# Between a graph layer and an attention layer: when weights are loaded, who fills a row of ones, and which product comes first

## The chip, the core and the metric

One NeuronCore of a Trainium2 chip. The metric is the device time of one execution in microseconds (us). Engines: PE (TensorE), DVE (VectorE), ACT (ScalarE), POOL (GpSimd) and SP (SyncE, which here only issues DMAs).

## The reference

A network of two graph blocks on 6250 nodes with 128 features and 206,250 edges sorted by target. The first block makes a message per edge, reduces the messages of each target (sum, squares, maximum, minimum), and applies two dense layers. The second is what matters here:

```python
h = x @ gcn_w                                   # graph layer (GCN)
out = zeros.at[dst].add(h[src] * norm[:, None])
h = silu(layernorm(out + gcn_b) )               # with gamma, beta
hh = (h @ gat_w).reshape(N, 2, 128)             # attention layer (GAT), 2 heads
a_src = sum(hh * att_src, -1);  a_dst = sum(hh * att_dst, -1)
e = leaky_relu(a_src[src] + a_dst[dst])
alpha = exp(e - m[dst]) / den[dst]              # m, den: maximum and sum over the edges of a target
out = mean over heads of sum(hh[src] * alpha);  x = layernorm(x + silu(layernorm(out + gat_b)))
```

## The kernel before

Nodes lie on the free axis, padded to 6400, in the large tile `acc` of 128 features x 5 planes x 6400. The program is a row of phases, each a block of five instruction streams; between two blocks all engines meet at a barrier, and after some phases POOL clears semaphores in a small block of its own (`recycle`).

- `phase_sum` is the graph layer: it adds scaled feature rows over the edges into plane 1 of `acc`. SP loads the row starts of the edge list (`rr`, L1217) and waits for DVE, which computes from them where the irregular windows begin (`s_jt`); then SP loads the edge indices (`meta`, L1228) by which POOL gathers rows (L1256).
- `phase_gcn` is the stage changed here. It turns plane 1 into the tables of the attention layer, in 13 groups of 512 nodes (the last has 256), 4 blocks of 128 each. SP loads seven small tiles (L1521 to L1526): `gw` (the graph layer's weight), `gwT` (the attention weight, transposed), `at` (two score weights) and `gb` (bias, gamma, beta on all partitions), all on one semaphore. PE first makes the score vectors (L1533, into `PV`, a corner of the PSUM tile `AB`), that is weight times score weight, and then per group: `q` the product with `gw` (L1541), `t` a transpose, `a` the scores (L1561, L1564). DVE first fills a row of ones on partition 32 of planes 3 and 4 (L1573; the attention layer keeps its running sum there), then copies the score vectors to SBUF and adds them (L1575, L1577), and then per group: `f1` scales and adds the bias (L1586), makes the statistics (L1590, L1593) and adds epsilon to the variance (L1595); `f2` normalises (L1602 to L1611) after ACT's square root; `gg` copies scores and takes the leaky maximum (L1627). ACT makes the square root, the SiLU, copies and stores. POOL has no instruction in it.
- `phase_gat` is the attention layer itself, 2100 us of gathers and products; it starts after a barrier.

The order within a stream is written out by hand: `steps(NG, [(lag, f), ...])` calls in step i every f for group i - lag. `Chain` counts DVE's instructions on a semaphore; `ch.sync()` waits for all of them, and `ch.raises(s)` signals s by a no-op behind them (L97).

Of the kernel before, what the change touches and what calls it, by code (L numbers as in the profile page):

```python
# [9 lines left out]
ALU = mybir.AluOpType  # L10
# [32 lines left out]
class Entry:  # L43
# [15 lines left out]
    def first(self, m):  # L59

        return isinstance(self.i, int) and self.i + self.o < m
# [38 lines left out]
def build(nc, d, out, upto=99):  # L100
    with ExitStack() as top:
        def sem(name):
            return top.enter_context(nc.semaphore(name))
# [39 lines left out]
        s_pool = sem("s_pool")  # L143
        s_sync = sem("s_sync")
        s_pad = sem("s_pad")


        with ExitStack() as ph:
# [251 lines left out]
        phase_n1(nc, d, locals())  # L400
        if upto < 3:
            return
        phase_sum(nc, d, locals())
        phase_gcn(nc, d, locals())
        if upto < 5:
            return
        phase_gat(nc, d, locals())
# [369 lines left out]
def steps(n, stages, before=None):  # L777

    for i in range(n + max(lag for lag, _ in stages)):
        if before is not None and i < n:  # L780
            before(i)
        for lag, f in stages:
            if 0 <= i - lag < n:
                f(i - lag)
# [343 lines left out]
def phase_sum(nc, d, v):  # L1128
# [12 lines left out]
    with ExitStack() as ph:  # L1141
# [73 lines left out]
        @blk.sync  # L1215
        def _(e):
            e.dma_start(rr[:, :], RPD[0:(NW + 1) * WD].rearrange("(a w k) -> a w k", a=1, k=WD)[:, :, 0],  # L1217
                        allow_slow_non_contiguous=True).then_inc(l_rr, 16)
            e.wait_ge(s_jt, 1)
            j0 = entry0(e)  # L1220

            def load(x):
                k = x.slot(4)
                c = e.value_load(tb[0:1, ds(nth(e, j0, x), 1)], min_val=0, max_val=NCH - 1)
                if not x.first(4):
                    wait_sync(e, l_g[k], 64 * x.uses(4, -1), s_sync)
                    wait_sync(e, s_oh, x.at(-3), s_sync)
                e.dma_start(meta[:, k, :], d["meta"][ds(c, 1), :, :].rearrange("a p s -> (a p) s")).then_inc(l_mt[k], 16)  # L1228

            for o in range(4):  # L1230
                load(Entry(0, o))
            e.wait_ge(s_lim, 1)
            e.dma_start(WTD.rearrange("(a k) n -> a k n", a=1), wt[:, :, :]).then_inc(l_wt, 16)
            e.wait_ge(l_wt, 16)
            e.dma_start(wc[:, :, :], WTD.rearrange("k (g p) -> p k g", p=128), allow_slow_non_contiguous=True).then_inc(l_wt, 16)
            with e.bass.Fori(4, entries(e), 4, engines=bass.OrderedEngineSet([e.engine])) as i:
                for o in range(4):
                    load(Entry(i, o))
# [232 lines left out]
def phase_gcn(nc, d, v):  # L1471
# [5 lines left out]
    TAB, ADT = v["TAB"], v["ADT"]  # L1477
    NG = len(GROUPS)
    with ExitStack() as ph:
        gw = sbt(ph, "gw", [128, 128])  # L1480
        gwT = sbt(ph, "gwT", [128, 2, 128])
        at = sbt(ph, "at", [128, 2, 2])
        gb = sbt(ph, "gb", [128, 3, 128])
        vv = sbt(ph, "vv", [128, 3, 2])
        tt = sbt(ph, "tt", [128, 2, 4, 128])
        zz = sbt(ph, "zz", [128, 2, 4, 128])
# [8 lines left out]
        AB = pst(ph, "AB", [128, 512])  # L1495
        LR = [pst(ph, f"LR{k}", [128, 512]) for k in range(2)]
        PV = AB[:, 500:504]
        w = sem("m_w")
        s_o = [sem(f"m_o{k}") for k in range(4)]
        s_pv = sem("m_pv")  # L1500
        s_vv = sem("m_vv")
# [14 lines left out]
            o, n = GROUPS[g]  # L1516
            return slice(o, o + n), n, n // 128

        @blk.sync
        def _(e):  # L1520
            e.dma_start(gw[:, :], d["gcnw"]).then_inc(w, 16)  # L1521
            e.dma_start(gwT[:, :, :], d["gatwT"].rearrange("(h c) f -> c h f", h=2)).then_inc(w, 16)
            e.dma_start(at[:, 0, :], d["atts"]).then_inc(w, 16)
            e.dma_start(at[:, 1, :], d["attd"]).then_inc(w, 16)
            for k, t in enumerate(("gcnb", "gamma", "beta")):
                e.dma_start(gb[:, k, :], d[t].partition_broadcast(128)).then_inc(w, 16)  # L1526

        @blk.tensor
        def _(e):
            e.wait_ge(w, 112)  # L1530
            for h in range(2):
                for k in range(2):
                    mm = e.matmul(PV[:, 2 * k + h:2 * k + h + 1], gwT[:, h, :], at[:, k, h:h + 1], start=True, stop=True)  # L1533
            mm.then_inc(s_pv, 1)

            def q(g):
                c, n, nb = cols(g)
                if g >= 2:
                    e.wait_ge(s_f1, g - 1)
                for b in range(nb):  # L1540
                    mm = e.matmul(Q[g % 2][:, b * 128:(b + 1) * 128], acc[:, 1, c.start + b * 128:c.start + (b + 1) * 128],  # L1541
                                  gw[:, :], start=True, stop=True)
                mm.then_inc(s_q, 1)

            def t(g):
                c, n, nb = cols(g)
                e.wait_ge(s_h, g + 1)
                if g >= 1:
                    e.wait_ge(s_c1, g)
                for b in range(nb):  # L1550
                    mm = e.transpose(HT[:, b * 128:(b + 1) * 128], ts[:, g % 4, b, 0:128], ident[:, :])
                mm.then_inc(s_t, 1)

            def a(g):
                c, n, nb = cols(g)
                e.wait_ge(s_c1, g + 1)
                e.wait_ge(s_vv, 1)
                if g >= 1:
                    e.wait_ge(s_g, g)
                for b in range(nb):  # L1560
                    e.matmul(AB[:, b * 4:b * 4 + 4], acc[:, 1, c.start + b * 128:c.start + (b + 1) * 128],  # L1561
                             vv[:, 0:2, :].rearrange("p k h -> p (k h)"), start=True, stop=True)
                for h in range(2):
                    mm = e.matmul(LR[h][0:1, 0:n], vv[:, 2, h:h + 1], acc[:, 1, c], start=True, stop=True)  # L1564
                mm.then_inc(s_ab, 1)

            steps(NG, [(0, q), (2, t), (3, a)])

        @blk.vector
        def _(e):  # L1570
            ch = Chain(e, s_v)
            e.wait_ge(w, 112)
            ch(e.memset(acc[32:33, 3:5, :], 1.0))  # L1573
            e.wait_ge(s_pv, 1)
            ch(e.tensor_copy(vv[:, 0:2, :].rearrange("p k h -> p (k h)"), PV[:, :]))  # L1575
            ch.sync()
            ch(e.tensor_tensor(vv[:, 2, :], vv[:, 0, :], vv[:, 1, :], ALU.add))  # L1577
            ch.raises(s_vv)

            def f1(g):  # L1580
                c, n, nb = cols(g)
                q = g % 2
                e.wait_ge(s_q, g + 1)
                for b in range(nb):
                    o = c.start // 128 + b
                    ch(e.scalar_tensor_tensor(tt[:, q, b, :], Q[q][:, b * 128:(b + 1) * 128], dinv[:, o:o + 1],  # L1586
                                              gb[:, 0, :], ALU.mult, ALU.add))
                ch.sync()
                for b in range(nb):
                    ch(e.bn_stats(bn[:, b, :], tt[:, q, b, :]))  # L1590
                ch.sync()
                for b in range(nb):
                    ch(e.bn_aggr(mv[:, q, b, :], bn[:, b, :]))  # L1593
                ch.sync()
                ch(e.tensor_scalar(rs[:, q, 0:nb], mv[:, q, 0:nb, 1], EPS, None, ALU.add))  # L1595
                ch.raises(s_f1)

            def f2(g):
                c, n, nb = cols(g)
                q = g % 2  # L1600
                e.wait_ge(s_rs, g + 1)
                ch(e.reciprocal(rs[:, q, 0:nb], rs[:, q, 0:nb]))  # L1602
                ch.sync()
                for b in range(nb):
                    ch(e.scalar_tensor_tensor(tt[:, q, b, :], tt[:, q, b, :], mv[:, q, b, 0:1], gb[:, 1, :],
                                              ALU.subtract, ALU.mult))
                ch.sync()
                if g >= 2:
                    e.wait_ge(s_h, g - 1)
                for b in range(nb):  # L1610
                    ch(e.scalar_tensor_tensor(zz[:, q, b, :], tt[:, q, b, :], rs[:, q, b:b + 1], gb[:, 2, :],  # L1611
                                              ALU.mult, ALU.add))
                ch.raises(s_f2)

            def gg(g):
                c, n, nb = cols(g)
                q = g % 2
                e.wait_ge(s_ab, g + 1)
                AV = AB[:, 0:4 * nb].rearrange("p (b k) -> p b k", k=4)
                q = g % 4  # L1620
                if g >= 4:
                    e.wait_ge(s_o[q], 32 * (g // 4))
                ch(e.tensor_copy(ts[:, q, 0:nb, 128:130], AV[:, :, 0:2]))
                ch(e.tensor_copy(adt[:, q, 0:nb, :], AV[:, :, 2:4]))
                e.wait_ge(s_lr, g + 1)
                for h in range(2):
                    ch(e.tensor_tensor(acc[0:1, 3 + h, c], lr[0:1, h, 0:n], LR[h][0:1, 0:n], ALU.max))  # L1627
                ch.raises(s_g)

            steps(NG, [(1, f2), (0, f1), (3, gg)])  # L1630

        @blk.scalar
        def _(e):
# [619 lines left out]
```

## Time and profile before

| | |
|---|---|
| median of 3 runs | 5772.62 us (5770.69 to 5776.23) |
| the profiled execution | 5773.65 us |
| its span, first to last instruction | 5771.7 us |
| mean granted clock of TensorE | 0.947 |
| PE, DVE, ACT, POOL busy | 88%, 83%, 50%, 67% |
| graph layer (`phase_sum`) | 2485 to 3385 us |
| stage changed (`phase_gcn`) | 3387 to 3520 us |
| attention layer | 3524 us to about 5625 us |

A row of the timeline gives the start and the length of an instruction (or of several alike, xN, merged), engine and line, the tiles written and read, and in brackets how long the engine stood idle before and what released it. SPq is SP's DMA issue. PE records: an fp32 product of one 128x128 block appears as two or more records. The granted clock is 1.0 at 2.4 GHz and 0.5 at 1.2 GHz.

### The profile page before, as it was taken

To read this page: it belongs to the slowest core of one execution; us is meant where nothing else is said; L and a number is where in the kernel's file an instruction comes from. 1 tells how busy PE (TensorE), PEld (TensorE's weight loads), DVE (VectorE), ACT (ScalarE), POOL (GpSimd) and SP (SyncE) were. 2 spreads that over 40 slices of the span, in tenths; PEclk is the share of its full clock that TensorE was granted. 3 is DMA by queue.
4 is the path that set the end of the run, shared out by engine and by line. 5 is a ranking of instruction groups with operands and counts; after the bars stand their busy time and mean duration, and the time that the engine had idled before them with its cause. 6 is when DMAs were issued, how large, how long until landed. Compare 5 with 4: busy or idle time off the path is not lost. (4 is left out here: it accounts for less than half of the span.)

```text
span 5771.7 us, 176467 instructions
## 1 busy us (share of the span) xinstructions
PE 5106.0 (88%) x41872; PEld 4051.2 (70%) x42482; DVE 4775.1 (83%) x12693; ACT 2880.1 (50%) x6715; POOL 3884.4 (67%) x3976
## 2 busy tenths in 40 slices
PE   3999999999999997968888866999999999999993
PEld 3888888888888886447777754666666666666663
DVE  4999999999999997767777756888888888888887
ACT  1565666656665654123333334555555555555556
POOL 2777777777777774047777724777777777777772
PEclk7999999999999998969888877999999999999996
DMA  6666666666666664322222212222222222222221
GB/s 156 160 159 159 157 158 156 159 156 158 157 157 157 158 157 119 99 53 54 54 54 53 54 33 43 54 53 53 54 53 53 53 53 53 53 53 53 53 53 48
DMA packets 667245, 544.72 MB, mean 94 GB/s; under 512 B 365794, under 2 KB 544171, under 8 KB 666853
## 3 DMA queue, kind: packets, MB, share of 16 engines
q0 software_dynamic: 126336, 262.13, 19.1%
q1 hardware_dynamic: 415050, 163.69, 12.4%
q10 hardware_dynamic: 125724, 117.57, 7.8%
q14 instruction: 108, 0.88, 0.1%
q8 instruction: 27, 0.44, 0.0%
HBM read 517.22 MB, written 25.61 MB: 94 GB/s over the span
## 5 line engine op out<-in xcount | busy, mean ns | idle before, releaser
L1766 POOL DMA_INDIRECT Gt<-TAB,metat x1632 | 1597.2, 979 | 646.9 <-issue 496.4
L559 POOL DMA_INDIRECT G<-Atab,ms x1616 | 1575.6, 975 | 576.9 <-issue 460.3
L1256 POOL DMA_INDIRECT Gc<-XS,metac x672 | 645.3, 960 | 241.8 <-issue 189.0
L1806 DVE SCALAR_TENSOR_TENSOR M<-neqt,Gt 128x256 f32<-128x256 f32 x816 | 311.0, 422 | 309.0 <-DMA Gt<-TAB,metat 308.8
L663 ACT COPY BS<-BK 128x512 f32<-128x512 f32 x808 | 465.6, 576 | 198.9 <-PE BK L752 191.1
L1401 ACT COPY acc<-CP 128x300 f32<-128x300 f32 x630 | 269.5, 428 | 555.1 <-PE CP L1439 552.4
L606 DVE TENSOR_TENSOR_SCAN ST<-mm,ST,ET 128x512 f32<-128x512 bf16 x404 | 516.7, 1279 | 0.1
L608 DVE TENSOR_TENSOR_SCAN ST<-mm,ST,ET 128x512 f32<-128x512 bf16 x404 | 506.9, 1255 | 0.0
L702 PE MATMUL Z<-WB,ZR 128*128 128x128 f32 x3232 | 429.3, 276 | 66.8 <-DVE ZR L577 66.6
L752 PE MATMUL BK<-ident,ST 128*128 128x128 f32 x3232 | 485.1, 273 | 2.4 <-ACT BS L663 1.8
L1970 PE MATMUL SR<-P,Gt 128*128 128x128 f32 x3264 | 473.7, 288 | 0.0
L1970 PEld LDWEIGHTS SR<-P,Gt 128*128 128x128 f32 x3264 | 395.8, 191 | 70.2 <-issue 70.2
L720 PE MATMUL S<-EE,oh 128*64 128x128 f32 x6464 | 442.5, 279 | 0.0
L702 PEld LDWEIGHTS Z<-WB,ZR 128*128 128x128 f32 x3232 | 428.5, 193 | 12.0
L1414 PE MATMUL OT<-acc 128*128 128x180 f32 x2100 | 431.7, 332 | 0.5 <-ACT acc L1401 0.5
L1904 ACT ACTIVATE EX<-TE,nl 128x512 f32<-128x512 f32 x408 | 294.7, 722 | 270.9 <-ACT nl L1897 140.2
L639 ACT ACTIVATE EE<-EE 128x512 f32<-128x512 f32 x404 | 255.1, 631 | 346.3 <-issue 273.1
L769 PE MATMUL S<-BS,oh 128*64 128x128 f32 x6464 | 422.5, 273 | 1.4 <-issue 1.4
L752 PEld LDWEIGHTS BK<-ident,ST 128*128 128x128 f32 x3232 | 392.6, 141 | 32.7 <-issue 2.5
L1327 DVE TENSOR_SCALAR O<-iotaD,VA 128x300 bf16<-128x300 f16 x1260 | 400.3, 322 | 1.0
L720 PEld LDWEIGHTS S<-EE,oh 128*64 128x64 f32 x6464 | 345.0, 137 | 67.7 <-issue 67.7
L1439 PE MATMUL CP<-O 128*128 128x300 bf16 x1260 | 301.2, 326 | 78.3 <-DVE O L1327 74.8
(291 smaller groups left out, 11448.5 us busy)
## 6 DMA issues: line engine op xcount, KB each, us to landing
mm<-MM ACTq DMA_DIRECT2D x404, 256.0 KB
ZR<-in_eft SPq DMA_DIRECT2D x404, 128.0 KB
dstb<-DF SPq DMA_DIRECT2D x404, 128.0 KB
Gt<-TAB,metat POOLq DMA_INDIRECT x1632
G<-Atab,ms POOLq DMA_INDIRECT x1616
ad<-ADT SPq DMA_DIRECT2D x816, 0.2 KB
WB<-Btab SPq DMA_DIRECT2D x404, 32.0 KB
Gc<-XS,metac POOLq DMA_INDIRECT x672
```

The source lines that it names most:

```text
L559: e.indirect_dma_start(G[:, k, s, :], None, Atab, bass.IndirectOffsetOnAxis(ap=ms[:, k, s:s + 1], axis=0)).then_inc(l_g[k], 16)
L606: e.tensor_tensor_scan(ST[:, q, 0, :], mm2[:, k, 0, :], ET[q][:, :], ST[:, 1 - q, 0, CH - 1:CH], ALU.mult, ALU.max)
L608: e.tensor_tensor_scan(ST[:, q, 1, :], mm2[:, k, 1, :], ET[q][:, :], ST[:, 1 - q, 1, CH - 1:CH], ALU.max, ALU.min).then_inc(s_d3, 1)
L663: e.copy(BS[:, q, a, :], BK[:, :]).then_inc(s_a2[a], 1)
L702: mm = e.matmul(Z[q][:, s * 128:(s + 1) * 128], ZR[:, k, s * 128:(s + 1) * 128], WB[:, k, :], start=True, stop=True)
L720: mm = e.matmul(S1[a * 64:(a + 1) * 64, 0:128], oh[:, k, s, :], EE[:, q, a, s * 128:(s + 1) * 128], start=(s == 0), stop=(s == 3))
L752: mm = e.transpose(BK[:, s * 128:(s + 1) * 128], ST[:, q, a, s * 128:(s + 1) * 128], ident[:, :])
L769: mm = e.matmul(S2[a * 64:(a + 1) * 64, 0:128], oh[:, k, 4 + s, :], BS[:, q, a, s * 128:(s + 1) * 128], start=(s == 0), stop=(s == 3))
L1256: e.indirect_dma_start(G[:, k, s, :], None, XS, bass.IndirectOffsetOnAxis(ap=meta[:, k, s:s + 1], axis=0)).then_inc(l_g[k], 16)
L1414: mm = e.matmul(OT[k][:, 0:DB], acc[:, 0, h * 128:(h + 1) * 128], C[k][:, h, :], start=(h == 0), stop=(h == NB - 1))
L1766: e.indirect_dma_start(G[:, k, s, :], None, TAB, bass.IndirectOffsetOnAxis(ap=meta[:, k, s:s + 1], axis=0)).then_inc(l_g[k], 16)
L1970: m = e.matmul(SR[q][:, 0:2 * W], G[:, k, s, 0:128], P[:, q, s * 128:(s + 1) * 128], start=(s == 0), stop=(s == 3))
```

## The change

The four weight tiles are allocated around both phases and loaded by SP in `phase_sum`, behind the load of the row starts. In `phase_gcn` the row of ones is filled by POOL, PE makes the first group's product before the score vectors, and DVE copies and adds these behind its first group.

```diff
@@ build
+        l_gw = sem("l_gw")
...
-        phase_sum(nc, d, locals())
-        phase_gcn(nc, d, locals())
+        with ExitStack() as mid:
+            gw = sbt(mid, "gw", [128, 128])
+            gwT = sbt(mid, "gwT", [128, 2, 128])
+            at = sbt(mid, "at", [128, 2, 2])
+            gb = sbt(mid, "gb", [128, 3, 128])
+            phase_sum(nc, d, locals())
+            phase_gcn(nc, d, locals())
@@ phase_sum, sync
             e.dma_start(rr[:, :], RPD[0:(NW + 1) * WD]...).then_inc(l_rr, 16)
+            e.dma_start(v["gw"][:, :], d["gcnw"]).then_inc(v["l_gw"], 16)
+            e.dma_start(v["gwT"][:, :, :], d["gatwT"].rearrange("(h c) f -> c h f", h=2)).then_inc(v["l_gw"], 16)
+            e.dma_start(v["at"][:, 0, :], d["atts"]).then_inc(v["l_gw"], 16)
+            e.dma_start(v["at"][:, 1, :], d["attd"]).then_inc(v["l_gw"], 16)
+            for k, t in enumerate(("gcnb", "gamma", "beta")):
+                e.dma_start(v["gb"][:, k, :], d[t].partition_broadcast(128)).then_inc(v["l_gw"], 16)
             e.wait_ge(s_jt, 1)
@@ phase_gcn
-        w = sem("m_w")
+        gw, gwT, at, gb, w = v["gw"], v["gwT"], v["at"], v["gb"], v["l_gw"]
+        s_one = sem("m_one")
...
-        @blk.sync
-        (the same seven loads)
+        @blk.gpsimd
+        def _(e):
+            e.memset(acc[32:33, 3:5, :], 1.0).then_inc(s_one, 1)
+            e.wait_ge(s_one, 1)
@@ tensor
             e.wait_ge(w, 112)
-            (the score vectors)
+            def score_vectors(): (the same)
...
-            steps(NG, [(0, q), (2, t), (3, a)])
+            def product(g):
+                q(g)
+                if g == 0:
+                    score_vectors()
+
+            steps(NG, [(0, product), (2, t), (3, a)])
@@ vector
             e.wait_ge(w, 112)
-            ch(e.memset(acc[32:33, 3:5, :], 1.0))
-            e.wait_ge(s_pv, 1)
-            ch(e.tensor_copy(vv[:, 0:2, :].rearrange("p k h -> p (k h)"), PV[:, :]))
-            ch.sync()
-            ch(e.tensor_tensor(vv[:, 2, :], vv[:, 0, :], vv[:, 1, :], ALU.add))
-            ch.raises(s_vv)
...
-            steps(NG, [(1, f2), (0, f1), (3, gg)])
+            def first(g):
+                f1(g)
+                if g == 0:
+                    (wait for s_pv, copy, add and signal as above)
+
+            steps(NG, [(1, f2), (0, first), (3, gg)])
```

DVE at the start of the stage, before:

```order
L1569 UNCONDITIONAL_BRANCH [waits barrier_Pool_Activation_PE_DVE_SP_release]
L1573 MEMSET acc 1x12800 [waits m_w]
L1575 COPY vv<-AB 128x4 [waits m_pv]
L1577 TENSOR_TENSOR vv<-vv 128x2 [waits m_v]
L97 ISA [waits m_v]
L1586 SCALAR_TENSOR_TENSOR tt<-Q,dinv,gb 128x128 [waits m_q]
```

The memset stands between the barrier and all that DVE does on a group. Now:

```order
L1591 SCALAR_TENSOR_TENSOR tt<-Q,dinv,gb 128x128 [waits m_q,l_gw]
L1591 SCALAR_TENSOR_TENSOR tt<-Q,dinv,gb 128x128 x3
L1595 BN_STATS bn<-tt 128x6 [waits m_v]
L1595 BN_STATS bn<-tt 128x6 x3
L1598 BN_AGGR mv<-bn 128x2 [waits m_v]
L1598 BN_AGGR mv<-bn 128x2 x3
L1600 TENSOR_SCALAR rs<-mv 128x4 [waits m_v]
L97 ISA [waits m_v]
L1639 COPY vv<-AB 128x4 [waits m_pv]
L1641 TENSOR_TENSOR vv<-vv 128x2 [waits m_v]
L97 ISA [waits m_v]
L1607 RECIPROCAL rs<-rs 128x4 [waits m_rs]
```

The memset is gone from DVE, and the copy and the addition stand between the first group's statistics and its reciprocal. (What is L1595 before the change is L1600 after it.) SP in the graph layer, now:

```order
L1223 DMA rrs<-RPD 1x631x1
L1225 DMA gw<-in_gcnw 128x128
L1226 DMA gwT<-in_gatwT 128x2x128
L1227 DMA at<-in_atts 128x2
L1228 DMA at<-in_attd 128x2
L1230 DMA gb<-in_gcnb 128x128
L1230 DMA gb<-in_gamma 128x128
L1230 DMA gb<-in_beta 128x128
L1198 TENSOR_LOAD jt [waits c_jt]
```

Seven issues stand between the load of the row starts and SP's wait for the table. POOL has the memset as its one instruction between two barriers.

## Rows read from the trace of the kernel before

**Rows 1.** The page: the span, and each engine's busy time

```profile
span 5771.7 us, 176467 instructions
...
PE 5106.0 (88%) x41872; PEld 4051.2 (70%) x42482; DVE 4775.1 (83%) x12693; ACT 2880.1 (50%) x6715; POOL 3884.4 (67%) x3976
```

**Rows 2.** Busy time by stretch: start:end length, PE, PEld, DVE, ACT, POOL, PEclk, DMA, GB/s

```profile
3387.00:3393.60 6.60, 0.00 (x0) 0.00 (x0) 0.00 (x0) 0.00 (x0) 0.00 (x0) 0.50 0.26 60
3393.60:3407.00 13.40, 5.49 (x24) 5.19 (x24) 10.71 (x1) 0.00 (x0) 0.00 (x0) 0.63 0.00 0
3407.00:3519.00 112.00, 77.11 (x286) 40.54 (x286) 82.14 (x331) 68.52 (x103) 0.00 (x0) 0.73 0.13 30
```

**Rows 3.** Timeline, start of attention tables: start, us, engine, line, tiles, [idle before]

```profile
3387.08 0.34 SPq L1521 DMA_DIRECT2D gw<-in_gcnw  x1
...
3389.87 0.43 SPq L1526 DMA_DIRECT2D gb<-in_beta  x1
...
3393.63 1.86 PE L1533 MATMUL AB<-at,gwT 128*128 128x1 f32 x8 [9.30 <-DMA gb<-in_beta]
...
3396.30 10.72 DVE L1573 MEMSET acc<- 1x12800 f32 x1 [11.15 <-issue]
3407.05 0.16 DVE L1575 COPY vv<-AB 128x4 f32<-128x4 f32 x1
...
3407.45 1.12 DVE L1586 SCALAR_TENSOR_TENSOR tt<-Q,dinv,gb 128x128 f32<-128x128 f32 x4
...
3409.93 0.17 DVE L1595 TENSOR_SCALAR rs<-mv 128x4 f32<-128x4 f32 x1
3410.18 0.21 ACT L1637 ACTIVATE rs<-rs 128x4 f32<-128x4 f32 x1 [58.94 <-DVEq L97]
...
3410.21 2.08 PE L1541 MATMUL Q<-gw,acc 128*128 128x128 f32 x8 [11.09 <-DVEq L97]
...
3410.42 0.18 DVE L1602 RECIPROCAL rs<-rs 128x4 f32<-128x4 f32 x1 [0.33 <-ACT rs L1637]
```

**Rows 4.** Timeline, the program's first stage: DVE beside POOL's memset

```profile
2.66 21.42 POOL L230 MEMSET acc<- 128x25600 f32 x1
14.27 10.03 DVE L304 CAST rows<-rowi 1x403 f32<-1x403 int32 x1 [14.15 <-DMA rowi<-in_lin]
24.23 0.34 DVE L305 CAST rows<-rowi 1x403 f32<-1x403 int32 x1
```

**Rows 5.** Timeline, the last stage: DVE beside a POOL operation

```profile
5743.08 1.26 POOL L2156 TENSOR_TENSOR yy<-zz,x 128x512 f32<-128x512 f32 x1 [2.91 <-ACT zz L2183]
...
5743.64 0.73 DVE L2095 TENSOR_SCALAR rs<-mv 128x4 f32<-128x4 f32 x1
...
5745.80 0.17 DVE L2095 TENSOR_SCALAR rs<-mv 128x4 f32<-128x4 f32 x1
```

**Rows 6.** Timeline, the start of the graph layer

```profile
2485.63 0.73 SPq L1217 DMA_DIRECT2D rrs<-RPD  x1
...
2485.96 0.38 POOL L1242 IOTA iotaD<- 128x300 f16 x1 [241.93 <-POOLq L789]
...
2491.29 0.47 DVE L1279 TENSOR_SCALAR rrs<-rrs 1x631 f32<-1x631 f32 x1 [4.21 <-DMA rrs<-RPD]
...
2499.30 3.92 SPq L1228 DMA_DIRECT2D metac<-in_meta  x4
```

**Rows 7.** DMA issues there: tile, queue, count, KB each, us to landing

```profile
gw<-in_gcnw SPq DMA_DIRECT2D x1, 64.0 KB, 1.8
...
gb<-in_beta SPq DMA_DIRECT2D x1, 64.0 KB, 3.7
```

**Rows 8.** Timeline, PE's row products near the end of the stage

```profile
3493.44 1.88 PE L1564 MATMUL LR<-acc,vv 128*1 128x512 f32 x4
...
3502.10 3.50 PE L1564 MATMUL LR<-acc,vv 128*1 128x512 f32 x4
```

More of the change, by code:

```diff
@@ L1479, in phase_gcn @@
     with ExitStack() as ph:
[L1480 to L1483, printed above, removed]
+        gw, gwT, at, gb, w = v["gw"], v["gwT"], v["at"], v["gb"], v["l_gw"]
         vv = sbt(ph, "vv", [128, 3, 2])
@@ L1517, in cols @@
             return slice(o, o + n), n, n // 128
-        @blk.sync
+        @blk.gpsimd
         def _(e):
[L1521 to L1526, printed above, removed]
+            e.memset(acc[32:33, 3:5, :], 1.0).then_inc(s_one, 1)
+            e.wait_ge(s_one, 1)
         @blk.tensor
@@ L1530, in _, with score_vectors @@
             e.wait_ge(w, 112)
[L1531 to L1534, printed above, removed]
+            def score_vectors():
+                for h in range(2):
+                    for k in range(2):
+                        mm = e.matmul(PV[:, 2 * k + h:2 * k + h + 1], gwT[:, h, :], at[:, k, h:h + 1], start=True, stop=True)
+                mm.then_inc(s_pv, 1)
             def q(g):
@@ L1628, in gg @@
                 ch.raises(s_g)
-            steps(NG, [(1, f2), (0, f1), (3, gg)])
+            def first(g):
+                f1(g)
+                if g == 0:
+                    e.wait_ge(s_pv, 1)
+                    ch(e.tensor_copy(vv[:, 0:2, :].rearrange("p k h -> p (k h)"), PV[:, :]))
+                    ch.sync()
+                    ch(e.tensor_tensor(vv[:, 2, :], vv[:, 0, :], vv[:, 1, :], ALU.add))
+                    ch.raises(s_vv)
+            steps(NG, [(1, f2), (0, first), (3, gg)])
         @blk.scalar
```

## The prediction

> **What bounds the kernel now.** I read the page first: engine shares of the whole span [rows 1]. PE and DVE are busy 88% and 83% of it, but the edit touches one short stage, so those shares say nothing of its worth. The busy time by stretch shows the stage [rows 2]: 6.6 us in which no engine does anything, 13.4 us in which DVE has one instruction, and then 112 us of real work on 13 groups. All engines pass a barrier at its start and at its end, so every microsecond saved in the first two stretches moves the end of the program, unless it comes back later. The timeline gives the chain of waits [rows 3]. SP issues its first weight load at 3387.08 and its last at 3389.87; PE starts at 3393.63, released by that last load; DVE's memset begins at 3396.30 and takes 10.72; then come the copy of the score vectors at 3407.05 and the first operation on a product at 3407.45. So DVE reaches its first useful work 20.4 us after SP's first issue: 6.55 (loads) + 2.67 (a wait that the trace gives to nobody) + 10.75 (memset) + 0.40 (copy and add).
>
> **The change part by part.** The sum is made against the profiled execution's own 5773.65 us; the median shown is 5772.62, 1.0 lower, and the predicted time starts from the median.
>
> *Weights loaded in the graph layer.* The seven issues leave this stage: -6.55 us, if nothing else takes their place. They are placed behind the row-start load on SP's queue and ahead of SP's wait for the window table. Here they took from 3387.08 to 3390.30 to issue [rows 3], 3.2 us; behind the row-start load, which ends at 2486.4, they end near 2489.6, and the first load of edge indices is only issued at 2499.30 [rows 6]. SP's queue is thus covered with 9.7 us to spare; without that cover each would cost its 0.46. Their transfers run beside the row-start load, for which DVE waits until 2491.29 [rows 6]. Bounds: nothing, as the first load of the seven landed in 1.8 us with six behind it, while the last needed 3.7 [rows 7]; or that DVE gets the row starts only after all seven have landed, 6.55 after 2486.4, thus 2492.9 in place of 2491.29, +1.7. I take 0, since the row-start load is first in its queue as the 1.8 us one was.
>
> *Product ahead of the score vectors.* PE's first four blocks take 2.08 us (eight records at the granted clock of 0.5, the 1.2 GHz level, like the row at 3410.21 [rows 3]; the stretch before has 0.50 too [rows 2]). With weights in place it starts with the stage, at about 3387.1, and DVE can start at about 3389.3. From there alone DVE would be 3407.45 - 3389.3 = 18.1 us early. The four score products (1.86 for eight records) run while DVE is on the first product, and the second group's products follow; both lie beside DVE's work.
>
> *Row of ones on POOL.* DVE loses 10.72 us of work, and the 2.67 before it. POOL does nothing in this stage [rows 2], and nobody waits for the row inside the stage, so its own time looks hidden. It is not. In the first stage a cast of 403 elements took 10.03 us beside POOL's memset, ending at 24.26, just after the memset's end at 24.08; the same form next to it took 0.34 [rows 4]. In the last stage a tensor_scalar of 4 elements took 0.73 beside a POOL operation that ended at 5744.34, and itself ended at 5744.37; alone it takes 0.17 [rows 5]. That instruction is the same as L1595, which closes the statistics of each group in the stage changed here: `rs<-mv`, 128x4. The Trainium skill (SBUF — State Buffer, Who interferes with whom) has this as a rule: a copy, cast or tensor_scalar in a two-port mode and a GpSimd instruction exclude each other for the whole instruction, and whichever is issued first wins; by it the change gains less than the trace of the stage alone suggests, and the two stretches agree.
>
> So POOL starts its memset when the stage starts, 0.33 after SP as in the graph layer [rows 6], at 3387.4. Its length: 25600 elements took 21.42 [rows 4], so 12800 take 10.7, to 3398.1. DVE does the four products' scaling and the statistics in 2.48 us (3407.45 to 3409.93 [rows 3]) and reaches the tensor_scalar at 3391.8. There it waits 6.3 us and ends 0.03 to 0.2 after the memset, at 3398.2. Before, it ended at 3410.10. **Gain so far: 11.9 us**, in place of 18.1. Queued behind it on DVE are the score-vector copy and all later groups; ACT's square root and PE's third product wait for it too.
>
> *Score-vector copy and add moved behind the first group.* They take 0.40 (3407.05 to 3407.45). Before, DVE waited 0.32 there for ACT's square root (3410.10 to 3410.42), which now covers most of it; with the signal to ACT ahead of them and one behind them, about 0.12 is left over: +0.1. PE needs the vectors only three steps later.
>
> *The rest.* The 112 us of 13 groups keep their order, and the end barrier finds POOL long done. Near the end of the stage PE's four row-product records took 3.50 us at the low clock, and 1.88 earlier at the high one [rows 8]; how the clock falls there once the start is different can't be read. The last two full groups and the half one wait for PE in part, which bounds a gain by 1.6 + 1.6 + 0.8 = 4 us; a loss is bounded near 0, as they already run mostly at the low clock. I take 0. Sum: -11.9 + 0.1 + 0 = **-11.8 us**: 5761.9 for a profiled execution, 5760.8 for the median.
>
> **The rivals.**
> - *Full gain.* The memset does not hold DVE up (one partition only, where rows 4 has 128; or the tensor_scalar of 4 elements is not of the kind that is held). Then DVE ends L1595 at 3389.3 + 2.65 = 3391.95: -18.0 us, 5754.6. Against it speak both stretches [rows 4, 5], of which the second is the very form. If the unexplained 2.67 us belongs to DVE's start and not to the memset, this case gives -15.4, 5757.2. Chance 0.12.
> - *The memset is longer than its row says.* On DVE the stretch from PE's start at 3393.63, on the same semaphore, to the next instruction at 3407.05 is 13.4 us, with a row of 10.72 in it [rows 3]; the row's 0.84 ns per element is also POOL's in rows 4. If POOL's real pace were 13.4 for 12800, it would end at 3400.8 and the gain be 9.2: 5763.4. Against it: POOL's row of 21.42 starts at 2.66 and the cast that it held was free at 24.26, and 26.8 us do not fit into that. The Trainium skill (VectorE: DVE Perf Modes, Zero memsets can be issued as uint32) says that a memset takes one cycle per element, and gives 0.96 GHz for VectorE: an estimate of 13.3 us, which would explain the 2.67 on DVE and says nothing of POOL's clock. Chance 0.08.
> - *A late start.* Row starts delayed by the added transfers (+1.7), or POOL or PE entering the stage 1 to 2 us later than assumed, of which only POOL's costs anything: about -10, 5762.6. Chance 0.08.
> - *Slower than before.* POOL fills one partition at the pace at which it adds two tensors, 1.26 us for 512 [rows 5], 2.5 ns per element: 31.5 us, to 3418.9. DVE would be held at L1595 until 3419, 9 us later than now: 5781.6. It decides from 22.7 us on, 1.77 ns per element. Against it: rows 4, 0.84. Chance 0.02.
> - *The change doesn't do what it says.* Nothing in the stage waits for a load any more except the weights, and they have 890 us to land; I see no way, and give it no chance of its own.
>
> **How the numbers follow.** My forecast has 0.70. Inside it lie the clock at the stage's end and how the 2250 us of attention behind it fall out, about 2 us either way. A measurement of this kernel can tell about 0.2%, 11.5 us, from no change, and the forecast of -11.8 stands almost on that bound: 0.62 of its chance is beyond it, since the clock's unknown leans to a gain. Faster: 0.70 x 0.62 + 0.12 = 0.55. Slower: 0.01, half of the last case. Same: 0.44. The range takes the forecast from -8 to -16 and reaches down to the full gain: 5754.5 to 5764.5; the slow case is left out, and about half of the long memset.
>
> **What would show it.** Right: PE's first product at 3387.1 to 3387.5 on the old scale; a POOL memset of 10.7 us from the start of the stage; one DVE tensor_scalar `rs<-mv` of about 6.4 us that ends with it, the other twelve at 0.17; seven issues in 3.3 us between the row-start load and the index loads, and the gap before the first graph-layer DVE operation still 4.2. Wrong: that first tensor_scalar at 0.17 (full gain), a memset of another length, or a stage of 112 us that is more than 2 us longer or shorter from that instruction to its end.

## The result

| | before | changed |
|---|---|---|
| median, 14 runs each | 5772.94 us (5768.49 to 5777.25) | 5759.18 us (5757.21 to 5766.00) |
| ratio | | 0.998, 95% interval 0.9973 to 0.9987 |
| the profiled execution | 5773.65 us | 5760.19 us |
| its span | 5771.7 us | 5758.1 us |

The change makes the kernel 13.8 us faster by the medians, 0.24%, and the interval of the ratio lies wholly under 1, by more than 0.1%. The forecast was 11.8 us, 5760.8. The page of the changed kernel, for [rows 1]:

```profile
span 5758.1 us, 177079 instructions
...
PE 5133.3 (89%) x42482; PEld 4048.9 (70%) x42482; DVE 4769.9 (83%) x12692; ACT 2880.2 (50%) x6715; POOL 3892.4 (68%) x3977
```

The shares of the whole span don't show the change, as expected. The timeline at the stage's start, for [rows 3]. Columns as there: start, us, engine, line, tiles, in brackets the idle time before. What was L1595, L1602, L1575 and L1586 is now L1600, L1607, L1639 and L1591:

```profile
3384.02 0.34 DVE L1345 TENSOR_TENSOR acc<-acc,OT 128x180 f32<-128x180 f32 x1
3386.32 10.76 POOL L1530 MEMSET acc<- 1x12800 f32 x1 [6.98 <-SPq L1491]
...
3386.36 2.05 PE L1547 MATMUL Q<-gw,acc 128*128 128x128 f32 x8 [2.81 <-PEq L795]
...
3388.53 1.12 DVE L1591 SCALAR_TENSOR_TENSOR tt<-Q,dinv,gb 128x128 f32<-128x128 f32 x4 [4.16 <-PE Q L1547]
...
3391.01 6.10 DVE L1600 TENSOR_SCALAR rs<-mv 128x4 f32<-128x4 f32 x1
3397.15 0.16 DVE L1639 COPY vv<-AB 128x4 f32<-128x4 f32 x1
...
3397.54 0.17 DVE L1607 RECIPROCAL rs<-rs 128x4 f32<-128x4 f32 x1
...
3402.58 0.17 DVE L1600 TENSOR_SCALAR rs<-mv 128x4 f32<-128x4 f32 x1
```

POOL's memset and PE's first product start together, 1.96 us after the graph layer's last DVE operation has ended. DVE is on the first product at 3388.53 and at its tensor_scalar at 3391.01. That one instruction is held: it takes 6.10 us and ends at 3397.11, 0.03 after POOL's memset (3397.08); the next of its form takes 0.17. The whole line says the same (minimum, median and maximum in ns):

```profile
L1600 DVE TENSOR_SCALAR rs<-mv x13: 169/170/6098, 3391.0 to 3483.4; 128x4 f32<-128x4 f32 x12, 128x2 f32<-128x2 f32 x1
```

I measure the stage's start from the graph layer's last DVE instruction (start) to the first reciprocal: before 3384.80 to 3410.42, 25.62 us; now 3384.02 to 3397.54, 13.52 us. That is 12.1 of the 13.6 us by which the spans differ. The graph layer ends 0.78 earlier in this execution, and the rest falls behind the stage. Its end and the start of the attention layer, changed kernel:

```profile
3489.09 3.57 PE L1570 MATMUL LR<-acc,vv 128*1 128x512 f32 x4
...
3497.03 3.57 PE L1570 MATMUL LR<-acc,vv 128*1 128x512 f32 x4
...
3503.72 1.02 PE L1570 MATMUL LR<-acc,vv 128*1 128x256 f32 x4
...
3511.29 0.11 DVE L1787 MEMSET zw<- 128x64 uint32 x1 [5.10 <-PEq L1491]
```

and the kernel before:

```profile
3509.43 3.25 PE L1564 MATMUL LR<-acc,vv 128*1 128x512 f32 x4
...
3515.88 1.86 PE L1564 MATMUL LR<-acc,vv 128*1 128x256 f32 x4
...
3524.24 0.11 DVE L1773 MEMSET zw<- 128x64 uint32 x1 [5.05 <-PEq L1479]
```

From the first reciprocal to that memset of the attention layer it is 113.75 us now and 113.82 before, although the granted clock at the stage's end did move: the last full group's row products now took 3.57 (granted clock 0.50) and the half group's 1.02 (0.96), where they took 3.25 (0.57) and 1.86 (0.50). Counted from the first reciprocal, the last full group's end 0.80 us later than before, and the half group's, which come last, 0.12 earlier. From that memset to the end of the span it is 2246.8 against 2247.5. The start of the graph layer, for [rows 6]:

```profile
2485.68 0.73 SPq L1223 DMA_DIRECT2D rrs<-RPD  x1
...
2486.46 3.88 SPq L1225 DMA_DIRECT2D gw<-in_gcnw  x1
...
2491.31 0.48 DVE L1291 TENSOR_SCALAR rrs<-rrs 1x631 f32<-1x631 f32 x1 [4.17 <-DMA rrs<-RPD]
...
2493.03 0.43 SPq L1230 DMA_DIRECT2D gb<-in_beta  x1
...
2499.31 3.88 SPq L1240 DMA_DIRECT2D metac<-in_meta  x4
```

DVE has the row starts 5.63 us after their issue, against 5.66 before, and the index loads are issued at 2499.31 against 2499.30. So the added loads cost nothing there. But the first of them kept SP's queue for 3.88 us, and the last was issued at 2493.03, not before 2489.6.

### The profile page after: what moved, and what is told of

The parts are those of the page before. It is cut to its first block and busy times, and to the rows that moved or that the text cites. A ratio compares the mean times of both kernels' runs of the same rounds, so it can differ in the third digit from the quotient of the medians.

```text
span 5758.1 us, 177079 instructions
## 1 busy us (share of the span) xinstructions
PE 5133.3 (89%) x42482; PEld 4048.9 (70%) x42482; DVE 4769.9 (83%) x12692; ACT 2880.2 (50%) x6715; POOL 3892.4 (68%) x3977
```

## The experiments

Twelve runs, each a set of executions or a single one, on three chips. On two of these chips the whole program took about 7930 us, with the runs of one kernel spread over 1%; there only the inside of the stage can be read, and its start agrees to 0.01 us with the first comparison: the changed kernel has 13.52 us from the graph layer's end to the first reciprocal in both. The third chip was like that of the first comparison (before: 5762.75 us, 9 executions). On it ran the two-input epsilon for the third time, "order back" and the two kernels that combine the two-input epsilon with a part undone. "Distance" below is always that from the graph layer's last DVE instruction to the first reciprocal. The kernel before was profiled only in the first comparison.

| kernel | distance, us | to the attention layer, us |
|---|---|---|
| before | 25.62 | 113.82 |
| changed | 13.52 | 113.75 |
| changed, again | 13.52 | 113.09 |
| two-input epsilon (three runs) | 7.59, 7.58, 7.58 | 114.09, 114.23, 113.11 |
| memset in 13 pieces | 7.58 | 113.19 |
| loads back in the stage | 13.81 | 112.72 |
| early loads alone | 19.15 | 113.64 |
| early loads, memset halved between DVE and POOL | 12.49 | 113.77 |
| two-input epsilon, POOL copies | 13.62 | 113.24 |
| order back | 13.41 | 113.29 |
| two-input epsilon, order back | 9.10 | 112.11 |
| two-input epsilon, loads in the stage | 13.82 | 112.93 |

The second column, from the first reciprocal to the attention layer's first memset, spreads by 2 us, and by 1.1 us within one kernel (the two-input epsilon); I see no edit that it follows.

**The changed kernel again.**

> The changed kernel again, as the reference for the runs beside it. Expected 13.8 us under the kernel before (5772.94 to 5759.18 in the runs already seen), with the first tensor_scalar of the stage held for about 6.1 us until POOL's memset ends.

Measured: 7917.3 us against 7932.4, ratio 0.9983 with an interval of 0.9959 to 1.0007, which takes in both the expected gain and none; the tensor_scalar took 6.10 us again.

**Two-input epsilon.** POOL's memset stays whole; only the held instruction changes its form.

```diff
-ch(e.tensor_scalar(rs[:, q, 0:nb], mv[:, q, 0:nb, 1], EPS, None, ALU.add))
+ch(e.scalar_tensor_tensor(rs[:, q, 0:nb], ones[:, 0:nb], EPS, mv[:, q, 0:nb, 1], ALU.mult, ALU.add))
```

> Epsilon is added by an instruction with two inputs in SBUF (ones times epsilon, plus the variance) in place of the tensor_scalar, in all 13 groups. Theory A (the tensor_scalar was held because its form and POOL's memset exclude each other, while a two-input instruction is not held by a POOL instruction that only writes): the instruction takes about 0.2 us in the first group too, the memset runs on beside it, and the kernel is 6 us faster than the changed one, 20 us under before. Rival B (any DVE instruction that writes to SBUF after the statistics is held by the memset, or the first one is late for a reason that has nothing to do with POOL): it still takes about 6 us, and the time stays at 13.8 us under before.

Timeline of this kernel:

```profile
4794.44 0.34 DVE L1345 TENSOR_TENSOR acc<-acc,OT 128x180 f32<-128x180 f32 x1
4796.73 10.76 POOL L1530 MEMSET acc<- 1x12800 f32 x1 [6.96 <-SPq L1491]
...
4801.43 0.16 DVE L1600 SCALAR_TENSOR_TENSOR rs<-ones,mv 128x4 f32<-128x4 f32 x1
...
4802.03 0.17 DVE L1608 RECIPROCAL rs<-rs 128x4 f32<-128x4 f32 x1
```

The instruction that adds epsilon takes 0.16 us while the memset runs on for another 5.9. Theory A holds: what is held is the form, not whatever DVE does there. End to end 7923.6 us, ratio 0.999 (0.9967 to 1.0014): the expected 20 us (0.9975) lie inside the interval, and so does no gain.

**Memset in pieces.**

```diff
-e.memset(acc[32:33, 3:5, :], 1.0).then_inc(s_one, 1)
-e.wait_ge(s_one, 1)
+for g in range(NG):
+    e.wait_ge(s_f1, g + 1)
+    e.memset(acc[32:33, 3:5, cols(g)[0]], 1.0).then_inc(s_one, 1)
+e.wait_ge(s_one, NG)
```

> POOL's memset in 13 pieces of 2x512, each after the signal that closes a group's statistics. Theory A: each piece takes 0.9 to 1.0 us and lies beside DVE instructions with two inputs, so that no tensor_scalar is held; the first one takes 0.17 us and the kernel is 6 us faster than the changed one, 20 us under before. Rival B (late for a reason other than POOL): the first tensor_scalar still takes 6 us and the time is that of the changed kernel. In-between: if pieces hit a copy or the two-input instructions too, some of the 13 groups get up to 1 us longer each, and up to all of the 6 us is lost.

```profile
4782.43 0.34 DVE L1345 TENSOR_TENSOR acc<-acc,OT 128x180 f32<-128x180 f32 x1
...
4789.41 0.17 DVE L1602 TENSOR_SCALAR rs<-mv 128x4 f32<-128x4 f32 x1
...
4789.69 0.94 POOL L1532 MEMSET acc<- 1x1024 f32 x1 [11.93 <-DVEq L97]
...
4790.01 0.17 DVE L1609 RECIPROCAL rs<-rs 128x4 f32<-128x4 f32 x1
```

Here the held instruction is untouched, and with POOL idle when it comes it takes 0.17; the 13 of its line take 0.17 on average, so no piece holds any of them. Both ways to part the two give the same 5.93 to 5.94 us. End to end 7928.7 us, ratio 0.9994 (0.9973 to 1.0015), unclear again; the expected 20 us would be 0.9975, near the interval's lower end.

**Loads back in the stage.** The seven loads leave `phase_sum` and are issued by SP in `phase_gcn`; POOL's memset and the order stay.

```diff
@@ phase_sum, sync
-e.dma_start(v["gw"][:, :], d["gcnw"]).then_inc(v["l_gw"], 16)
...
@@ phase_gcn
+@blk.sync
+def _(e):
+    e.dma_start(gw[:, :], d["gcnw"]).then_inc(w, 16)
...
```

> Only the loads are undone: SP loads the seven tiles in the stage again, POOL's memset and the new order stay. PE then starts 6.55 us later, at 3392.9 on the changed kernel's scale, DVE reaches the tensor_scalar at about 3397.6, and POOL's memset ended at 3397.08. Theory A: the loads were hidden behind the hold but for 0.7 us, so the time is 13 us under before. Rival C (the loads carry their own 6.5 us of the gain): 7.3 us under before.

```profile
4797.36 0.34 DVE L1339 TENSOR_TENSOR acc<-acc,OT 128x180 f32<-128x180 f32 x1
...
4799.65 10.76 POOL L1533 MEMSET acc<- 1x12800 f32 x1 [6.95 <-POOLq L795]
...
4805.89 2.07 PE L1550 MATMUL Q<-gw,acc 128*128 128x128 f32 x8 [9.01 <-DMA gb<-in_beta]
...
4810.56 0.17 DVE L1603 TENSOR_SCALAR rs<-mv 128x4 f32<-128x4 f32 x1
...
4811.17 0.17 DVE L1610 RECIPROCAL rs<-rs 128x4 f32<-128x4 f32 x1
```

The weights arrive 6.2 us after the stage's start, PE and DVE are late by all of it, and it costs 0.29 us: DVE reaches the tensor_scalar 0.15 after POOL's memset has ended. Under the hold the early loads were worth 0.3 us of the stage, not 6.5. (End to end 7930.9 us, ratio 0.9997, 0.998 to 1.0015, which tells nothing.)

**Two-input epsilon, a second time.**

> The kernel with the two-input epsilon once more, because in the earlier call the whole program took 7930 us on its chip with runs spread over 1%, against 5773 us, and 6 us can't be seen there. Inside the stage the runs agreed to 0.01 us: from the graph layer's last DVE instruction to the first reciprocal 25.62 us in the kernel before, 13.52 in the changed one, 7.59 here. Theory A (what the stage gains arrives at the end of the program): 12.1 + 5.9 plus the 0.8 to 1.5 us that the changed kernel gained outside the stage, so 18 to 20 us under before, on a chip as in the first comparison. Rival (the attention layer gives some back): 14 us or less.

7912.3 us, ratio 0.9982 (0.9962 to 1.0003): the distance is 7.58 again. On these two chips the ratios of the kernels without the hold (0.999, 0.9994, 0.9982) all lie nearer to 1 than the expected 0.9975. Each interval still takes 0.9975 in, and whether the stage's gain arrives at the end there is not shown.

**Early loads alone.** DVE's memset is back, ahead of everything, and so are copy and addition; PE makes the score vectors first; POOL has nothing.

```diff
@@ vector
 e.wait_ge(w, 112)
+ch(e.memset(acc[32:33, 3:5, :], 1.0))
+e.wait_ge(s_pv, 1)
+ch(e.tensor_copy(vv[:, 0:2, :]..., PV[:, :]))
...
-steps(NG, [(1, f2), (0, first), (3, gg)])
+steps(NG, [(1, f2), (0, f1), (3, gg)])
@@ tensor
+score_vectors()
-steps(NG, [(0, product), (2, t), (3, a)])
+steps(NG, [(0, q), (2, t), (3, a)])
```

> Only the early loads of the change: DVE's memset, then the score vectors' copy, then the first group, and PE's score vectors first, as in the kernel before. Measured from the graph layer's last DVE instruction to the first reciprocal (25.62 us before). Theory D1 (the memset occupies DVE for 13.4 us although its row says 10.72): 19.1 us, so 6.5 under before. Theory D2 (the memset takes 10.72 and 2.67 is a late start that belongs to the wait for the weights): 16.4, so 9.2 under before. In either case the row reads 10.72.

```profile
4793.49 0.34 DVE L1345 TENSOR_TENSOR acc<-acc,OT 128x180 f32<-128x180 f32 x1
...
4795.82 1.84 PE L1535 MATMUL AB<-at,gwT 128*128 128x1 f32 x8 [2.81 <-PEq L795]
...
4798.51 10.72 DVE L1576 MEMSET acc<- 1x12800 f32 x1 [4.68 <-issue]
4809.27 0.16 DVE L1578 COPY vv<-AB 128x4 f32<-128x4 f32 x1
...
4812.64 0.18 DVE L1605 RECIPROCAL rs<-rs 128x4 f32<-128x4 f32 x1 [0.33 <-ACT rs L1640]
```

19.15 us, as theory D1 gives. The weights are long there, yet the memset's row still begins 2.69 us after PE's, and 13.45 us pass from PE's start to the copy. The late start does not belong to the wait for the weights. Early loads alone save 6.5 us of the stage. End to end 7918.9 us, ratio 0.9978 (0.9955 to 1.0001).

**Memset halved.** As the run above, with `acc[32:33, 3, :]` on DVE and `acc[32:33, 4, :]` on POOL.

> As the run with early loads alone, but DVE fills half of the row (6400 elements) and POOL the other half at the same time. Same distance, to the first reciprocal. Theory D1 (a memset costs DVE 1.04 us per 1000 elements): 6.7 us in place of 13.4, so 12.4 us. Theory D3 (10.72 by its row for 12800, and a fixed late start of 2.67 at the stage's beginning): 5.4 + 2.7, so 13.7 us. Both kernels' POOL part ends before DVE's tensor_scalar and holds nothing; should it hold DVE's memset, DVE ends 5.4 us later than under D1.

```profile
4823.73 0.34 DVE L1345 TENSOR_TENSOR acc<-acc,OT 128x180 f32<-128x180 f32 x1
4826.03 5.42 POOL L1530 MEMSET acc<- 1x6400 f32 x1 [7.06 <-SPq L1491]
...
4826.07 1.84 PE L1539 MATMUL AB<-at,gwT 128*128 128x1 f32 x8 [2.81 <-PEq L795]
4827.42 5.39 DVE L1580 MEMSET acc<- 1x6400 f32 x1 [3.35 <-issue]
...
4832.85 0.16 DVE L1582 COPY vv<-AB 128x4 f32<-128x4 f32 x1
...
4836.22 0.18 DVE L1609 RECIPROCAL rs<-rs 128x4 f32<-128x4 f32 x1 [0.33 <-ACT rs L1644]
```

The row is half as long (5.39), and so is the "late start", 1.35 us in place of 2.69. A fixed late start would have kept 2.7. From PE's start to the copy it is 6.78 us for 6400 elements and 13.45 for 12800: 1.04 ns for each further element, of which the row shows 0.83. The distance, 12.49, is theory D1's 12.4. The two memsets ran side by side without holding each other. (One run, 7961.5 us.)

**POOL reads.** The two-input epsilon kernel, with a POOL copy in place of the memset:

```diff
-e.memset(acc[32:33, 3:5, :], 1.0).then_inc(s_one, 1)
+e.tensor_copy(acc[32:33, 3:5, :], ones[32:33, 0:1].unsqueeze(2).to_broadcast([1, 2, NP])).then_inc(s_one, 1)
```

> The two-input epsilon kernel, with POOL filling the row by a copy that reads a tile of ones, in place of a memset that reads nothing. Its length is unknown: 10.7 us at one element per cycle, up to 31.5 at POOL's pace with two inputs. Theory A (an instruction with two SBUF inputs and a POOL instruction that reads SBUF exclude each other): the instruction that adds epsilon, 0.16 us beside the memset, is held until POOL's copy ends, and the stage gets longer than the changed kernel's. Rival B2 (two-input instructions are never held by POOL's work of this kind): 0.16 us and 7.6 us to the first reciprocal as in the kernel with the memset.

```profile
4781.79 0.34 DVE L1345 TENSOR_TENSOR acc<-acc,OT 128x180 f32<-128x180 f32 x1
...
4784.11 10.84 POOL L1530 COPY acc<-ones 1x12800 f32<-1x12800 f32 x1 [6.99 <-SPq L1491]
...
4786.29 1.13 DVE L1591 SCALAR_TENSOR_TENSOR tt<-Q,dinv,gb 128x128 f32<-128x128 f32 x4 [4.16 <-PE Q L1547]
...
4788.77 6.20 DVE L1600 SCALAR_TENSOR_TENSOR rs<-ones,mv 128x4 f32<-128x4 f32 x1
...
4795.41 0.17 DVE L1608 RECIPROCAL rs<-rs 128x4 f32<-128x4 f32 x1
```

The same instruction that took 0.16 beside a memset now takes 6.20 and ends with POOL's copy. The first operation of the group, whose large input is in PSUM, is not held (1.13 for four, as ever). So the form that escapes a POOL write does not escape a POOL read. In this run both instructions also read the tile `ones`, so that the shared tile could be the cause. The last stage of the kernel before speaks against it. There POOL reads `tt` and `tu`, DVE reads another buffer of `tt` and `gb`, and four two-input instructions take 1.83 us beside POOL and 1.14 with POOL idle:

```profile
5738.91 1.26 POOL L2148 TENSOR_TENSOR tt<-tt,tu 128x512 f32<-128x512 f32 x1 [3.09 <-ACT tu L2170]
...
5739.27 1.83 DVE L2120 SCALAR_TENSOR_TENSOR tt<-tt,mv,gb 128x128 f32<-128x128 f32 x4
...
5754.63 1.14 DVE L2120 SCALAR_TENSOR_TENSOR tt<-tt,mv,gb 128x128 f32<-128x128 f32 x4
```

I had left the length open and expected the stage to become longer than the changed kernel's; it is by 0.1 us, since the copy takes 10.84. (One run, 7922.1 us.)

**Two-input epsilon, a third time**, now on a chip like the first.

> The two-input epsilon kernel a third time, for the end-to-end time. If the chip is like the one of the first comparison: 18 to 20 us under before. If it is like that of the earlier experiments, where the runs of one kernel spread over 1%, three sets together should put the ratio at 0.9975 (20 of 7930) within about 0.001; the rival that the gain is given back behind the stage puts it at 0.9982 or above.

5740.84 us (5738.68 to 5745.84, 5 runs) against 5762.75 (5761.02 to 5768.14, 9 runs): 21.9 us, ratio 0.9964, interval 0.9951 to 0.9978. In microseconds the interval is 13 to 28: the rival's 0.9982 lies outside it, the rival's 14 us of the second run just inside. The slowest execution here is 15.2 us under the fastest of the kernel before, so most of the gain does arrive at the end. The distance gives 18.0 us of it. Whether the other 3.9 us are the edit's or the spread's is open; the interval takes in 18. No other kernel has a shorter distance; the memset in pieces has the same, and neither it nor the changed kernel was run on this chip.

**Order back.** Early loads and POOL's memset stay; PE makes the score vectors first, and DVE copies and adds before its first group.

> Only the order is undone: PE makes the score vectors first, DVE copies and adds them before its first group; early loads and POOL's memset stay. To the first reciprocal 25.62 us before, 13.52 in the changed kernel. Theory A: the first product comes 1.7 us later but DVE still reaches the tensor_scalar before POOL's memset ends; held to the same time, and without copy and addition behind it the reciprocal comes 0.1 earlier: 13.4 us. Rival C (each part carries its own gain): 15.2 us.

```profile
3381.17 10.76 POOL L1530 MEMSET acc<- 1x12800 f32 x1 [6.96 <-SPq L1491]
...
3387.48 4.47 DVE L1601 TENSOR_SCALAR rs<-mv 128x4 f32<-128x4 f32 x1
...
3392.28 0.18 DVE L1608 RECIPROCAL rs<-rs 128x4 f32<-128x4 f32 x1 [0.33 <-ACT rs L1643]
```

The first group starts 1.6 us later, the hold is shorter by that much (4.47 against 6.10), and the distance is 13.41, 0.1 less. (One run, 5747.2 us.)

**Two-input epsilon with the order back.**

> The order undone as well, in the kernel with the two-input epsilon (7.59 us to the first reciprocal). Theory A: with nothing held, PE's 1.7 us ahead of the product are now on the path, less the 0.1 behind the statistics: 9.2 us. If the new order were worth nothing there either: 7.5 us.

9.10 us against 7.58: with nothing held the new order is worth 1.5 us. (One run, 5752.2 us.)

**Two-input epsilon with the loads in the stage.**

> The early loads undone, in the kernel with the two-input epsilon. Theory A: the loads' 6.2 us, of which 0.3 were visible under the hold, are all on the path: 13.8 us to the first reciprocal, as in the kernel with the loads in the stage and the tensor_scalar (13.81).

13.82 us, against 7.58 with early loads: 6.2 us, in place of the 0.3 under the hold. (One run, 5749.7 us.)

## Why the prediction was right

*What bounds it.* Right. The gain was to be found in 20 us between two barriers, and the 112 us behind stayed as they were.

*The hold.* Right, and it decided the size. Forecast: the first tensor_scalar reached at 3391.8, held 6.3 us, ended at 3398.2 on the old scale. Measured: reached at 3391.01, held to 3397.11. With the 0.78 by which the graph layer ended earlier, that is 3391.8 and 3397.9. It was read from [rows 4] and [rows 5] (by its row the cast of [rows 4] ends at 24.30, not at 24.26; the reading stands), and two edits that each leave the other side alone remove it for the same 5.9 us. The rule cited from the Trainium skill (SBUF — State Buffer, Who interferes with whom) agrees with these runs, and so does its finer part, which I did not use: an instruction with two SBUF inputs is held by a GpSimd instruction that reads SBUF, not by one that only writes; here 6.20 us beside a copy, 0.16 beside a memset. The rule speaks of a tensor_scalar in a two-port mode; no row names the mode in which an instruction ran, so this part of it is not shown.

*POOL's memset.* Its length is right, 10.76 for 10.7. The step that was off is its start: I took 0.33 us behind SP's first instruction from [rows 6], and it starts together with PE. That is 0.3 us earlier on the old scale, the difference between 11.9 and 12.2 us at the tensor_scalar. The rival in which it takes 13.4 fell with the row and the release 0.03 us after its end.

*Weights.* No cost in the graph layer, as taken (bound +1.7, measured -0.03 at the row starts). But "behind the row-start load they end near 2489.6" was wrong: the first issue took 3.88 us, the last ended at 2493.5, and the seven took 7.0 us where 3.3 was to be a sign of being right. The cover of 9.7 us became 5.8 and still sufficed.

*Copy and addition.* Right: +0.12 forecast, and the way back gives -0.11 (13.52 to 13.41).

*The unexplained 2.67 us.* I left it between two owners. It belongs to the memset: the row leaves out a fifth of what the instruction costs. The 20.4 us lost in the kernel before were 6.55 of loads, 13.4 of memset and 0.4 of copy. The Trainium skill (VectorE: DVE Perf Modes, Zero memsets can be issued as uint32) has one cycle per element; with the 0.96 GHz of that page (Specifications) the estimate was 13.3 us, and the runs show 13.4.

*The rest.* Sum -11.8; in the two profiles -12.1 in the stage's start, -0.1 in its groups, and -1.4 outside the stage (0.78 before, 0.65 behind), which no experiment ties to an edit. They are small beside what differs from run to run: the graph layer ended anywhere from 3378.77 to 3385.35 us in the four kernels profiled on the third chip, and the three of these that have the same graph layer span all of it. The medians differ by 13.8. The forecast of 11.8 stood almost on my bound of 11.5 us for telling a gain from no change; that the measured difference lies clearly beyond that bound is owed to what came from outside the stage, and that part was luck.

*What each part is worth.* The parts don't add up, since they hide behind one another. Undone alone in the changed kernel, they cost: loads 0.3 us, order -0.1. Undone alone where nothing is held: loads 6.2, order 1.5. Added alone to the old kernel the loads give 6.5.

## What to carry to other kernels

Work moved to an idle engine was not free here, since its instruction held one of the busy engine. Before moving a long POOL operation beside DVE, list the DVE instructions that will meet it and look in the trace for one of the same form beside POOL. Where one is held, change its form, or cut the POOL operation and place the pieces where no such instruction comes; either gave 5.9 us of the stage here, on top of the 12.1 of the change. And when several waits lie side by side, price each part with the others in place: under the hold the early loads were worth 0.3 us, without it 6.2.

## What was not expected of the hardware

- A DVE memset's row is too short. 12800 elements on one partition: row 10.72 us, 13.45 from PE's start to the next DVE instruction; 6400: 5.39 and 6.78. The missing time shows as idle time ahead of the row. POOL's memset rows (10.76 and 5.42) have no such gap.
- The first DMA issue behind the strided load of 631 single values took 3.88 us on SP's queue, the others 0.43 to 0.67; in the stage itself, with no such load ahead, the same issue took 0.34. That the strided load is the cause was not tested.
- A POOL memset and a DVE memset of 6400 elements each ran side by side, and neither held the other.
- On two chips the kernel before took 7932 and 7938 us, and in the other two sets of executions 5763 and 5773, with a mean granted clock of 0.85 and of 0.95. The start of this stage took the changed kernel 13.52 us on a chip of either kind. Why the whole program differs so much is open.
